# A normalise, shift and blur kernel whose second half takes its units in another order

## The chip, the cores and the metric

One core of one Trainium2 chip. The metric is the device time of one execution in microseconds (us), given as the median of several runs. Engines: TensorE (PE), VectorE (DVE), ScalarE (ACT), GpSimd (POOL), SyncE (SP).

## The reference

The input x is 32 images of 384 channels of 64 x 64 values in float32 (201 MB). It is normalised in groups of 12 channels, each channel group of 8 is moved by its own offset, blurred by a 3 x 3 kernel, and added to x:

```python
x = x + _L0_conv_ref(_gn(x), L0_conv_offset)
# _gn:   32 groups of 12 channels: (g - mean) / sqrt(var + 1e-5)
# _conv: off_round = round(offset); out = shift of each of 48 positions (8 channels) by off_round,
#        zeros where nothing comes in; then a depthwise 3x3 blur, its weights
#        exp(-(dx*dx + dy*dy) / 0.5), normalised, dx and dy from the offset's fraction
```

The 48 positions are a 7 x 7 grid of shifts, each 0, 16, 32 or 48 pixels up, down, left or right, without the centre. What remains of an image after a shift is a rectangle of (64 - |x|) x (64 - |y|) values, between 256 and 3072. Outside it (and its border) the output is x.

## The kernel before

**Tiles.** A tile is one position for 16 images: 128 partitions (16 images x 8 channels) of 4096 values, 2.10 MB. There are 48 positions and two halves of 16 images, so 96 tiles (`ALL`). SBUF holds 10 of them (`SLOTS`); tile n lies in slot n % 10, is loaded, updated in place and stored from there.

**Units.** The groups of 12 channels reach over the borders of positions; three neighbouring positions (24 channels) close two groups. So three tiles form a unit (`UNIT`), and a tile can't be normalised before all three tiles of its unit are loaded and summed. There are 16 units a half, 32 in all. A unit is named by its place in the program (units 16 to 31 are the second half).

**Order.** `positions_in_order` (L53) sorts the 16 units by the number of values that remain after the shift (`area`), takes the eight small and the eight large by turns, and swaps the last two. The list has 48 entries and both halves use it: places 0 to 47 and 48 to 95 (`ORDER[n % TILES]`). The sizes of its units, in order, each as the sizes of three tiles:

| place in the half | tiles | place | tiles |
|---|---|---|---|
| 0 | 256, 512, 768 | 8 | 1024, 768, 512 |
| 1 | 2304, 1536, 768 | 9 | 1024, 2048, 3072 |
| 2 | 768, 512, 256 | 10 | 1024, 512, 768 |
| 3 | 3072, 2304, 1536 | 11 | 1536, 2048, 1536 |
| 4 | 256, 512, 1024 | 12 | 768, 512, 1024 |
| 5 | 1536, 2304, 3072 | 13 | 1536, 2048, 1536 |
| 6 | 1024, 512, 256 | 14 | 768, 1536, 2304 |
| 7 | 3072, 2048, 1024 | 15 | 512, 768, 1024 |

**POOL** issues every load and store of x and out as an indirect DMA, with the rows from the table `row_of` (L182 to L202). It loads ten tiles, then for every n: wait until DVE has finished tile n, store it, wait until store n-1 has landed, load tile n+9 into that slot. All of these transfers go through one queue.

**ACT** (L226 on) makes two passes over each tile, the sum (L239) and the sum of squares about the mean (L243), except for tiles 0 and 2, which DVE sums; after the first tile of the next unit it takes the root for the unit before (L251), for which it waits for the matmuls of the variance.

**PE** adds the sums over the partitions of a group with a mask (L213): one set for the mean and one for the variance of each unit.

**DVE** does the rest of a tile, in `row_taps` (L380) and `column_tap` (L420): an edge to zero (L390), the normalised and shifted rectangle (L393), two row taps (L409, L414), and three column taps that add into the tile (L436, and L434 twice). Its time follows the size. In `run` (L439) the small steps of the next unit's statistics are placed among these:

```python
if j == UNIT - 2 and u < ALL_UNITS:
    spread_of_unit(u)
...
if j == UNIT - 1 and u < ALL_UNITS:
    scale_of_unit(u)
```

so in the second tile of a unit, after its first column tap, DVE waits for the next unit's means and makes the variance; and in the third tile, before its last tap, it waits for the root. A value read from memory sends the kernel down this branch when the offsets round to the planned grid, as they do here; the other branch (`displace`) serves other offsets.

Of the kernel before, what the change touches and what calls it, by code (L numbers as in the profile page):

```python
# [17 lines left out]
B, C, H, W = 32, 384, 64, 64  # L18
# [4 lines left out]
CH = C // POSITIONS  # L23
GROUP = C // 32
BT = 128 // CH
CHUNKS = B // BT
UNIT = 3
UNITS = POSITIONS // UNIT
TILES = UNITS * UNIT
# [6 lines left out]
SMALL = 7  # L36
MOVES = 1 + W + 2 + H
# [9 lines left out]
def planned_offsets():  # L47

    n = GRID // 2
    return [(ix * STRIDE, iy * STRIDE) for iy in range(-n, n + 1) for ix in range(-n, n + 1) if ix or iy]  # L50


def positions_in_order():  # L53

    def area(unit):
        return sum((W - abs(x)) * (H - abs(y)) for x, y in planned_offsets()[UNIT * unit:UNIT * (unit + 1)])

    units = sorted(range(UNITS), key=area)
    small, large = units[:UNITS // 2], units[UNITS // 2:]

    large = large[:1] + large[:1:-1] + large[1:2]
    order = [unit for pair in zip(small, large) for unit in pair]

    order[-2:] = order[:-3:-1]
    return [UNIT * unit + j for unit in order for j in range(UNIT)]


def span(shift, size):

    return max(0, shift), size + min(0, shift)  # L70
# [8 lines left out]
def norm_shift_blur(nc, x, offset, planned, steps, masks, rows, out):  # L79
    f32, i32, u32, u8 = mybir.dt.float32, mybir.dt.int32, mybir.dt.uint32, mybir.dt.uint8  # L80
    ALU = mybir.AluOpType
    ACT = mybir.ActivationFunctionType
    AX = mybir.AxisListType
    ORDER = positions_in_order()
    PLAN = planned_offsets()
    NP = POSITIONS
# [5 lines left out]
    with ctx:  # L92
# [169 lines left out]
        def _(dve):  # L262
# [77 lines left out]

            def scale_of_unit(u):

                par, base, p = u % 2, u * SMALL, ORDER[UNIT * u % TILES]

                dve.wait_ge(std_done, u + 1)
                nc.vector.reciprocal(rstd[:], std[:, par]).then_inc(small_done, 1)  # L346
                dve.wait_ge(small_done, base + 5)
                nc.vector.tensor_tensor(scale[:, par, :], rstd[:], middle[:, p:p + UNIT],  # L348
                                        ALU.mult).then_inc(small_done, 1)
                dve.wait_ge(small_done, base + 6)  # L350
                nc.vector.tensor_tensor(shift[:, par, :], scale[:, par, :], nmean[:],  # L351
                                        ALU.mult).then_inc(small_done, 1)

            def displace(n):

                g, t = normed, rowblur
                base, p = n * MOVES, ORDER[n % TILES]

                dve.wait_ge(col_taps, 1 + n * COL_TAPS)
                nc.vector.memset(t[:], 0.0).then_inc(moved, 1)  # L360
                with dve.Fori(0, W) as c:
                    to = dve.value_load(target[p:p + 1, 0, bass.ds(c, 1)], min_val=0, max_val=W + 1)

                    dve.wait_ge(moved, base + 1 + c)
                    nc.vector.tensor_scalar(t[:, :, bass.ds(to, 1)], g[:, 1:1 + H, bass.ds(c + 1, 1)], 1.0, None,
                                            ALU.mult).then_inc(moved, 1)

                dve.wait_ge(moved, base + 1 + W)
                nc.vector.memset(t[:, :, 0:W + 2:W + 1], 0.0).then_inc(moved, 1)
                nc.vector.memset(g[:], 0.0).then_inc(moved, 1)  # L370
                with dve.Fori(0, H) as r:
                    to = dve.value_load(target[p:p + 1, 1, bass.ds(r, 1)], min_val=0, max_val=H + 1)

                    dve.wait_ge(moved, base + 3 + W + r)
                    nc.vector.tensor_scalar(g[:, bass.ds(to, 1), :], t[:, bass.ds(r, 1), :], 1.0, None,
                                            ALU.mult).then_inc(moved, 1)

                dve.wait_ge(moved, base + MOVES)

            def row_taps(n, general):  # L380
                i, j = divmod(n, UNIT)
                p = ORDER[n % TILES]
                ox, oy = (0, 0) if general else PLAN[p]
                (xa, xb), (ya, yb) = span(ox, W), span(oy, H)
                image = tiles[:, n % SLOTS, :].rearrange("p (y x) -> p y x", x=W)

                dve.wait_ge(row_taps_done, 1 + n)
                if not general:
                    col = xa if xa > 0 else 1 + xb
                    nc.vector.memset(normed[:, 1 + ya:1 + yb, col:col + 1], 0.0).then_inc(edge_done, 1)  # L390

                dve.wait_ge(small_done, (i + 1) * SMALL)
                nc.vector.tensor_scalar(normed[:, 1 + ya:1 + yb, 1 + xa:1 + xb],  # L393
                                        image[:, ya - oy:yb - oy, xa - ox:xb - ox],
                                        scale[:, i % 2, j:j + 1], shift[:, i % 2, j:j + 1],
                                        ALU.mult, ALU.add).then_inc(normed_done, 1)
                dve.wait_ge(normed_done, n + 1)
                if general:
                    displace(n)
                else:  # L400
                    dve.wait_ge(edge_done, n + 1)
                g = normed[:, 1 + ya:1 + yb]
                t = rowblur[:, ya:yb]

                dve.wait_ge(col_taps, 1 + n * COL_TAPS)

                near = 1 if xb == W else -1
                ea, eb = max(0, xa - 1), min(W, xb + 1)
                nc.vector.scalar_tensor_tensor(t[:, :, 1 + ea:1 + eb], g[:, :, 1 + ea + near:1 + eb + near],  # L409
                                               ratio[:, (near + 1) // 2, p, 0:1], g[:, :, 1 + ea:1 + eb],  # L410
                                               ALU.mult, ALU.add).then_inc(first_row_tap, 1)
                fa, fb = max(0, xa + near), min(W, xb + near)
                dve.wait_ge(first_row_tap, n + 1)
                nc.vector.scalar_tensor_tensor(t[:, :, 1 + fa:1 + fb], g[:, :, 1 + fa - near:1 + fb - near],  # L414
                                               ratio[:, (1 - near) // 2, p, 0:1], t[:, :, 1 + fa:1 + fb],
                                               ALU.mult, ALU.add).then_inc(row_taps_done, 1)

                dve.wait_ge(row_taps_done, n + 2)

            def column_tap(n, general, nth):  # L420
                p = ORDER[n % TILES]
                ox, oy = (0, 0) if general else PLAN[p]
                (xa, xb), (ya, yb) = span(ox, W), span(oy, H)
                ea, eb = max(0, xa - 1), min(W, xb + 1)
                image = tiles[:, n % SLOTS, :].rearrange("p (y x) -> p y x", x=W)
                tap = (0, -1, 1)[nth]

                ra, rb = max(0, ya - tap), min(H, yb - tap)
                y = image[:, ra:rb, ea:eb]
                t = rowblur[:, ra + tap:rb + tap, 1 + ea:1 + eb]  # L430
                if nth:

                    dve.wait_ge(col_taps, 1 + n * COL_TAPS + nth)
                    ins = nc.vector.scalar_tensor_tensor(y, t, ratio[:, (tap + 1) // 2, p, 1:2], y, ALU.mult, ALU.add)  # L434
                else:
                    ins = nc.vector.tensor_tensor(y, t, y, ALU.add)  # L436
                ins.then_inc(col_taps, 1)

            def run(general):  # L439
                spread_of_unit(0)  # L440
                scale_of_unit(0)
                for n in range(ALL):
                    u, j = n // UNIT + 1, n % UNIT
                    row_taps(n, general)
                    column_tap(n, general, 0)
                    if j == UNIT - 2 and u < ALL_UNITS:
                        spread_of_unit(u)
                    column_tap(n, general, 1)
                    if j == UNIT - 1 and u < ALL_UNITS:
                        scale_of_unit(u)  # L450
                    column_tap(n, general, 2)
# [34 lines left out]
```

## Time and profile before

| | us |
|---|---|
| median of 3 runs | 989.47 |
| lowest, highest | 986.73, 991.32 |
| the profiled execution | 984.86 |
| its span | 983.1 |
| busy: DVE | 871.3 (89%) |
| busy: ACT | 714.3 (73%) |
| busy: POOL | 324.8 (33%) |
| busy: PE | 201.4 (20%) |
| read from and written to memory | 201.90 MB, 201.33 MB |
| mean rate over the span | 410 GB/s |

The span runs from the first to the last thing that the profiler records; times in the rows are from its start. An engine's busy time leaves out waits. POOL's busy time is the time in which it writes the descriptors of its DMAs; the transfer runs after that, and a row on a DMA issue doesn't show it. Transfers are seen in the DMA share and in GB/s.

### The profile page before, as it was taken

The page shows a single profiled execution, that of the slowest core. Times are in us where ns is not written, and L with a number is a line of the kernel's source. Part 1 is how long each engine was busy: PE and PEld are TensorE (multiplying, and loading weights), DVE is VectorE, ACT ScalarE, POOL GpSimd, SP SyncE. Part 2 cuts the span into 40 slices and gives each one's busy share as a digit, 9 for nine tenths or more (in the row PEclk, how much of TensorE's full clock was granted, in tenths as well). Part 3 has the DMA queues.
Part 4 walks back from the last instruction along what each step waited for, and adds up shares of the span by engine and source line. Part 5 has one row for each costly group of instructions (what it writes and reads, how often), then busy time and mean ns, then how long its engine had stood idle before and what let it go on. Part 6 is the DMA issues. An engine that isn't in the chain of part 4 may idle for free.

```text
span 983.1 us, 3636 instructions
## 1 busy us (share of the span) xinstructions
PE 201.4 (20%) x896; PEld 195.9 (20%) x896; DVE 871.3 (89%) x940; ACT 714.3 (73%) x412; POOL 324.8 (33%) x196
## 2 busy tenths in 40 slices
PE   0232222212122122122211221311212202222110
PEld 0221222212122122122211221311212202222110
DVE  4479899999999999999838949989999999979994
ACT  2998959777598777686777787686778777777800
POOL 3022342543323434223222317326141353223211
DMA  8999999999999999999999999999999999999966
GB/s 323 428 397 417 418 415 418 425 420 423 423 426 417 417 427 416 417 419 421 405 427 429 426 429 404 418 413 412 415 432 427 422 399 419 429 416 431 423 297 278
DMA packets 28233, 403.48 MB, mean 410 GB/s; under 512 B 3506, under 2 KB 3506, under 8 KB 3634
## 3 DMA queue, kind: packets, MB, share of 16 engines
q0 software_dynamic: 27648, 402.67, 98.2%
q1 hardware_dynamic: 562, 0.57, 0.2%
q8 instruction: 7, 0.11, 0.0%
q14 instruction: 16, 0.13, 0.0%
HBM read 201.90 MB, written 201.33 MB: 410 GB/s over the span
## 4 chain that ended last, share of the span: by engine, by line
DMA 54%; DVE 30%; issue 6%; POOL 5%; ACT 4%; PE 0%; POOLq 0%; ACTq 0%
DMA out<-tiles,row_of 48%; DVE tiles L434 10%; DMA tiles<-x,row_of 5%; DVE rowblur L409 5%; DVE tiles L436 5%; DVE rowblur L414 5%; POOL tiles L184 5%; ACT unread L239 3%; DVE normed L393 3%; ACT unread L243 1%; PE var_ps L213 0%; DMA row_of<-rows 0%; DVE scale L348 0%; DVE shift L351 0%; DVE apart L332 0%
## 5 line engine op out<-in xcount | busy, mean ns | idle before, releaser
L239 ACT ACTIVATE unread<-tiles 128x4096 uint8<-128x4096 f32 x94 | 339.9, 3616 | 165.2 <-DMA tiles<-x,row_of 164.7
L243 ACT ACTIVATE unread<-tiles,nmean_p 128x4096 uint8<-128x4096 f32 x94 | 348.7, 3709 | 3.0
L184 POOL DMA_INDIRECT tiles<-x,row_of x96 | 155.9, 1624 | 504.2 <-DMA out<-tiles,row_of 498.9
L434 DVE SCALAR_TENSOR_TENSOR tiles<-rowblur,ratio,tiles 128x272 f32<-128x272 f32 (+15 forms) x192 | 300.0, 1562 | 4.6
L213 PE MATMUL mean_ps<-nmean_p,mask 128*128 128x1 f32 x448 | 100.7, 353 | 567.3 <-ACT unread L239 537.2
L189 POOL DMA_INDIRECT out<-tiles,row_of x96 | 168.7, 1757 | 142.6 <-DVE tiles L434 119.7
L213 PEld LDWEIGHTS mean_ps<-nmean_p,mask 128*128 128x128 f32 x448 | 98.0, 330 | 570.0 <-ACT unread L239 539.8
L409 DVE SCALAR_TENSOR_TENSOR rowblur<-normed,ratio 128x272 f32<-128x272 f32 (+9 forms) x96 | 152.2, 1586 | 3.4
L436 DVE TENSOR_TENSOR tiles<-rowblur,tiles 128x272 f32<-128x272 f32 (+9 forms) x96 | 146.5, 1526 | 3.3
L414 DVE SCALAR_TENSOR_TENSOR rowblur<-normed,ratio,rowblur 128x240 f32<-128x240 f32 (+9 forms) x96 | 145.4, 1515 | 3.4
L213 PE MATMUL var_ps<-var_p,mask 128*128 128x1 f32 x448 | 100.7, 353 | 169.0 <-DVE var_p L338 169.0
L213 PEld LDWEIGHTS var_ps<-var_p,mask 128*128 128x128 f32 x448 | 98.0, 330 | 171.7 <-DVE var_p L338 171.7
L393 DVE TENSOR_SCALAR normed<-tiles,scale,shift 128x768 f32<-128x768 f32 (+6 forms) x96 | 87.3, 909 | 0.0
L251 ACT ACTIVATE std<-var_ps,eps 128x3 f32<-128x3 f32 x32 | 8.0, 252 | 50.8 <-PE var_ps L213 50.8
L329 DVE TENSOR_SCALAR nmean<-mean_ps 128x3 f32<-128x3 f32 x32 | 5.0, 155 | 37.2 <-PE mean_ps L213 37.2
L346 DVE RECIPROCAL rstd<-std 128x3 f32<-128x3 f32 x32 | 5.5, 171 | 27.1 <-ACT std L251 27.1
L312 DVE BATCH_NORM_STATS2 pieces<-tiles 128x6 f32<-128x512 f32 x16 | 9.7, 678 | 8.9 <-DMA tiles<-x,row_of 8.9
L239 ACT ACTIVATION_READ_ACCUMULATOR unread<-tiles 128x1 f32 x94 | 17.6, 187 | 0.0
L243 ACT ACTIVATION_READ_ACCUMULATOR unread<-tiles,nmean_p 128x1 f32 x94 | 17.5, 186 | 0.0
L390 DVE MEMSET normed<- 128x16 f32 (+3 forms) x96 | 8.5, 88 | 0.0
L338 DVE SCALAR_TENSOR_TENSOR var_p<-m_p,apart 128x3 f32<-128x3 f32 x32 | 5.2, 161 | 1.9 <-ACT unread L243 0.5
L351 DVE TENSOR_TENSOR shift<-scale,nmean 128x3 f32<-128x3 f32 x32 | 5.2, 164 | 1.1
(34 smaller groups left out, 25.9 us busy)
## 6 DMA issues: line engine op xcount, KB each, us to landing
tiles<-x,row_of POOLq DMA_INDIRECT x96, 14.9
out<-tiles,row_of POOLq DMA_INDIRECT x96, 17.6
mask<-masks SPq DMA_DIRECT2D x1, 448.0 KB, 3.2
row_of<-rows SPq DMA_DIRECT2D x1, 48.0 KB, 1.9
offs<-offset SPq DMA_DIRECT2D x1, 48.0 KB
plan_sb<-planned SPq DMA_DIRECT2D x1, 0.4 KB
offs_p<-offset SPq DMA_DIRECT2D x1, 0.4 KB
steps_sb<-steps SPq DMA_DIRECT2D x1, 12.0 KB
```

Source lines behind the costliest of these rows:

```text
L184: pool.indirect_dma_start(tiles[:, n % SLOTS, :], None, x_rows, bass.IndirectOffsetOnAxis(ap=row_of[:, n:n + 1], axis=0)).then_inc(loaded[ ...
L189: pool.indirect_dma_start(out_rows, bass.IndirectOffsetOnAxis(ap=row_of[:, n:n + 1], axis=0), tiles[:, n % SLOTS, :], None).then_inc(store ...
L213: last = nc.tensor.matmul(ps[:, k:k + 1], mask[:, PAIRS.index((j, k)), :], src[:, j:j + 1], start=(j == from_[0]), stop=(j == from_[-1]))
L239: nc.scalar.activation(unread[:], tiles[:, n % SLOTS, :], ACT.Identity, scale=-1.0 / HW, accum_out=nmean_p[:, i % 2, j:j + 1]).then_inc(nm ...
L243: nc.scalar.activation(unread[:], tiles[:, n % SLOTS, :], ACT.Square, bias=nmean_p[:, i % 2, j:j + 1], accum_out=m2_p[:, i % 2, j:j + 1]). ...
L312: nc.vector.bn_stats(pieces[:, e, :], tile[:, e, :]).then_inc(pieces_done, 1)
L390: nc.vector.memset(normed[:, 1 + ya:1 + yb, col:col + 1], 0.0).then_inc(edge_done, 1)
L393: nc.vector.tensor_scalar(normed[:, 1 + ya:1 + yb, 1 + xa:1 + xb], image[:, ya - oy:yb - oy, xa - ox:xb - ox], scale[:, i % 2, j:j + 1], s ...
L409: nc.vector.scalar_tensor_tensor(t[:, :, 1 + ea:1 + eb], g[:, :, 1 + ea + near:1 + eb + near], ratio[:, (near + 1) // 2, p, 0:1], g[:, :, ...
L414: nc.vector.scalar_tensor_tensor(t[:, :, 1 + fa:1 + fb], g[:, :, 1 + fa - near:1 + fb - near], ratio[:, (1 - near) // 2, p, 0:1], t[:, :, ...
L434: ins = nc.vector.scalar_tensor_tensor(y, t, ratio[:, (tap + 1) // 2, p, 1:2], y, ALU.mult, ALU.add)
L436: ins = nc.vector.tensor_tensor(y, t, y, ALU.add)
```

## The change

The second half gets a list of its own. The large units come in falling order of size, each followed by a small one, also falling; the last two large ones (4608 values each) come one after the other, and the two smallest (1536 each) are last. In the order of places 16 to 31 the tiles are: 1536, 2304, 3072; 512, 768, 1024; 3072, 2304, 1536; 768, 512, 1024; 1024, 2048, 3072; 1024, 512, 768; 3072, 2048, 1024; 1024, 768, 512; 1536, 2048, 1536; 1024, 512, 256; 1536, 2048, 1536; 256, 512, 1024; 768, 1536, 2304; 2304, 1536, 768; 768, 512, 256; 256, 512, 768. The list returned has 96 entries, so the modulo goes, and the table of rows is made from the same list. The first half is as before. The added lines shift the line numbers below them by 3.

```diff
@@ -62,6 +62,9 @@
     order = [unit for pair in zip(small, large) for unit in pair]
 
     order[-2:] = order[:-3:-1]
+
+    small, large = small[::-1], sorted(large, key=area)[::-1]
+    order += [unit for pair in zip(large[:-2], small[:-2]) for unit in pair] + large[-2:] + small[-2:]
     return [UNIT * unit + j for unit in order for j in range(UNIT)]
...
-                par, base, p = u % 2, u * SMALL, ORDER[UNIT * u % TILES]
+                par, base, p = u % 2, u * SMALL, ORDER[UNIT * u]
...
             def row_taps(n, general):
                 i, j = divmod(n, UNIT)
-                p = ORDER[n % TILES]
+                p = ORDER[n]
...
             def column_tap(n, general, nth):
-                p = ORDER[n % TILES]
+                p = ORDER[n]
...
-        "rows": np.stack([(chunk * BT + batch) * C + CH * p + ch for chunk in range(CHUNKS)
-                          for p in positions_in_order()], axis=1).astype(np.uint32),
+        "rows": np.stack([(n // TILES * BT + batch) * C + CH * p + ch
+                          for n, p in enumerate(positions_in_order())], axis=1).astype(np.uint32),
```

(`displace` is changed like `row_taps`.)

What moves on DVE, at the two places of which the prediction speaks. First the start of the second half, tile 48 and the start of tile 49, before and then after the change (the last number is the shape: partitions x rows x columns):

```order
L390 MEMSET normed 128x16
L393 TENSOR_SCALAR normed<-tiles,scale,shift 128x16x16
L409 SCALAR_TENSOR_TENSOR rowblur<-normed,ratio 128x16x17
L414 SCALAR_TENSOR_TENSOR rowblur<-normed,ratio,rowblur 128x16x15
L436 TENSOR_TENSOR tiles<-rowblur,tiles 128x16x17
L434 SCALAR_TENSOR_TENSOR tiles<-rowblur,ratio,tiles 128x16x17
L434 SCALAR_TENSOR_TENSOR tiles<-rowblur,ratio,tiles 128x15x17
```

```order
L393 MEMSET normed 128x48
L396 TENSOR_SCALAR normed<-tiles,scale,shift 128x48x32
L412 SCALAR_TENSOR_TENSOR rowblur<-normed,ratio 128x48x33
L417 SCALAR_TENSOR_TENSOR rowblur<-normed,ratio,rowblur 128x48x31
L439 TENSOR_TENSOR tiles<-rowblur,tiles 128x48x33
L437 SCALAR_TENSOR_TENSOR tiles<-rowblur,ratio,tiles 128x48x33
L437 SCALAR_TENSOR_TENSOR tiles<-rowblur,ratio,tiles 128x47x33
```

The same six steps and the memset stand there; a tile of 256 values a partition has given its place to one of 1536, and 2304 and 3072 follow where 512 and 768 did. Second the end of DVE's list, from the last tap of tile 92 into tile 93, before and after:

```order
L348 TENSOR_TENSOR scale<-rstd,middle 128x3
L351 TENSOR_TENSOR shift<-scale,nmean 128x3
L434 SCALAR_TENSOR_TENSOR tiles<-rowblur,ratio,tiles 128x48x49
L390 MEMSET normed 128x16
L393 TENSOR_SCALAR normed<-tiles,scale,shift 128x16x32
L409 SCALAR_TENSOR_TENSOR rowblur<-normed,ratio 128x16x33
```

```order
L351 TENSOR_TENSOR scale<-rstd,middle 128x3
L354 TENSOR_TENSOR shift<-scale,nmean 128x3
L437 SCALAR_TENSOR_TENSOR tiles<-rowblur,ratio,tiles 128x16x17
L393 MEMSET normed 128x16
L396 TENSOR_SCALAR normed<-tiles,scale,shift 128x16x16
L412 SCALAR_TENSOR_TENSOR rowblur<-normed,ratio 128x16x17
```

Tile 92 was one of 2304 (48 x 48) and is one of 256 (16 x 16); tile 93 was one of 512 and is one of 256. The small steps of the last unit's statistics stand before the last tap of tile 92 as they did. ACT, PE and POOL have the same instructions in the same order; only the rows in the table that POOL's transfers use are others.

## Rows read from the trace of the kernel before

**Rows 1.** The page: busy time by engine, GB/s in 40 slices, the POOL-issued queue

```profile
PE 201.4 (20%) x896; PEld 195.9 (20%) x896; DVE 871.3 (89%) x940; ACT 714.3 (73%) x412; POOL 324.8 (33%) x196
...
GB/s 323 428 397 417 418 415 418 425 420 423 423 426 417 417 427 416 417 419 421 405 427 429 426 429 404 418 413 412 415 432 427 422 399 419 429 416 431 423 297 278
...
q0 software_dynamic: 27648, 402.67, 98.2%
```

**Rows 2.** Waits: who waited for whom, in total, times, longest, POOL on the queue

```profile
POOL tiles L184 <- DMA out<-tiles,row_of: 498.9, 86, 9.4
```

**Rows 3.** Windows of the tail: stretch, busy by engine, clock, DMA share, GB/s

```profile
930.00:945.00 15.00, 6.29 (x28) 6.12 (x28) 14.69 (x14) 4.05 (x3) 1.95 (x1) 1.00 1.02 435
947.00:955.00 8.00, 0.00 (x0) 0.00 (x0) 7.83 (x10) 0.00 (x0) 1.01 (x1) 1.00 0.08 33
955.00:970.00 15.00, 0.00 (x0) 0.00 (x0) 14.54 (x18) 0.00 (x0) 2.43 (x2) 1.00 0.99 419
970.00:977.00 7.00, 0.00 (x0) 0.00 (x0) 0.57 (x1) 0.00 (x0) 0.95 (x1) 1.00 0.71 300
```

**Rows 4.** Timeline of POOL's last stores: start, duration, what, idle before and releaser

```profile
953.48 1.01 POOL L189 DMA_INDIRECT out<-tiles,row_of  x1 [13.12 <-DVE tiles L434]
...
970.85 0.95 POOL L189 DMA_INDIRECT out<-tiles,row_of  x1 [5.91 <-DVE tiles L434]
```

**Rows 5.** Timeline of DVE, the step that opens a tile (L393), second half

```profile
496.16 0.39 DVE L393 TENSOR_SCALAR normed<-tiles,scale,shift 128x256 f32<-128x256 f32 x1
...
583.81 1.83 DVE L393 TENSOR_SCALAR normed<-tiles,scale,shift 128x3072 f32<-128x3072 f32 x1
...
617.95 1.03 DVE L393 TENSOR_SCALAR normed<-tiles,scale,shift 128x1536 f32<-128x1536 f32 x1
...
628.60 0.40 DVE L393 TENSOR_SCALAR normed<-tiles,scale,shift 128x256 f32<-128x256 f32 x1
...
707.44 1.81 DVE L393 TENSOR_SCALAR normed<-tiles,scale,shift 128x3072 f32<-128x3072 f32 x1
...
748.11 0.80 DVE L393 TENSOR_SCALAR normed<-tiles,scale,shift 128x1024 f32<-128x1024 f32 x1
...
766.43 0.74 DVE L393 TENSOR_SCALAR normed<-tiles,scale,shift 128x1024 f32<-128x1024 f32 x1
```

**Rows 6.** Timeline of POOL's stores: third tile of units 16, 18, 22

```profile
542.82 1.58 POOL L189 DMA_INDIRECT out<-tiles,row_of  x1 [0.30 <-issue]
...
604.55 3.11 POOL L189 DMA_INDIRECT out<-tiles,row_of  x1 [0.30 <-issue]
...
724.24 3.71 POOL L189 DMA_INDIRECT out<-tiles,row_of  x1 [0.30 <-issue]
```

**Rows 7.** Timeline of POOL: a store that waited for DVE in the first half

```profile
266.05 1.28 POOL L189 DMA_INDIRECT out<-tiles,row_of  x1 [4.30 <-DVE tiles L434]
```

**Rows 8.** Timeline of DVE and ACT: statistics of units 29 and 31

```profile
874.09 0.16 DVE L329 TENSOR_SCALAR nmean<-mean_ps 128x3 f32<-128x3 f32 x1 [3.86 <-PE mean_ps L213]
...
933.75 0.15 DVE L329 TENSOR_SCALAR nmean<-mean_ps 128x3 f32<-128x3 f32 x1
...
937.78 0.26 ACT L251 ACTIVATE std<-var_ps,eps 128x3 f32<-128x3 f32 x1 [4.00 <-PE var_ps L213]
```

**Rows 9.** Timeline of DVE, the step that opens a tile, tail

```profile
938.11 1.43 DVE L393 TENSOR_SCALAR normed<-tiles,scale,shift 128x2304 f32<-128x2304 f32 x1
...
953.14 0.53 DVE L393 TENSOR_SCALAR normed<-tiles,scale,shift 128x512 f32<-128x512 f32 x1
...
957.50 0.66 DVE L393 TENSOR_SCALAR normed<-tiles,scale,shift 128x768 f32<-128x768 f32 x1
...
963.32 0.80 DVE L393 TENSOR_SCALAR normed<-tiles,scale,shift 128x1024 f32<-128x1024 f32 x1
```

**Rows 10.** Timeline of POOL's loads: the slowest stretch of the second half, first and last

```profile
589.88 3.46 POOL L184 DMA_INDIRECT tiles<-x,row_of  x1 [7.48 <-DMA out<-tiles,row_of]
...
642.60 0.97 POOL L184 DMA_INDIRECT tiles<-x,row_of  x1 [9.44 <-DMA out<-tiles,row_of]
```

More of the change, by code:

```diff
@@ L356, in displace @@
                 g, t = normed, rowblur
-                base, p = n * MOVES, ORDER[n % TILES]
+                base, p = n * MOVES, ORDER[n]
                 dve.wait_ge(col_taps, 1 + n * COL_TAPS)
```

## The prediction

> 0.5% of the time, about 5 us, is what a measurement of this kernel can tell from no change: the three runs of before spread from 986.73 to 991.32 us.
>
> **What bounds the kernel now.** I read the page first. VectorE (DVE) is busy 871.3 us (89%), yet the queue that GpSimd (POOL) fills moves 402.67 MB and its packets take 98.2% of the 16 DMA engines' span, and the rate holds between 397 and 432 GB/s from the second slice on until it falls to 297 and 278 in the last two [rows 1]. So the reader should see two things: the transfers set the pace, and only the end leaves them idle. The waits agree: POOL spends 498.9 us, in 86 pieces, waiting for stores to land before it may reload their slot [rows 2]. POOL's last load falls within this pace, and from 930 us the queue holds stores alone. Cut finely, the tail reads: 435 GB/s until 945, 33 GB/s from 947 to 955 while DVE is busy 7.83 of 8 us, 419 from 955 to 970, 300 from 970 to 977 [rows 3]. The hole is one large tile: POOL stood 13.12 us before it could issue the store at 953.48, because DVE was on a tile of 2304 elements a partition from 938.11 to 953.14 [rows 4, 9]. The last store, at 970.85, again waited 5.91 us for DVE [rows 4]. At the end, therefore, DVE is the bound; before it, the queue.
>
> **The change, part by part.**
>
> *Work added or removed: none.* Each half holds the same 48 tiles; each load and each store is 2.10 MB whatever the position; DVE's durations depend on the tile alone. The indices ORDER[n] are folded into the code when it is built. The statistics, the matmuls and POOL's list read the same, so everything rests on when DVE finishes a tile against when the queue wants it.
>
> *The tail.* What the queue still has to carry at 947 is four stores and the end of a fifth: 8.0 x 33 + 15.0 x 419 + 7.0 x 300 = 8.65 MB [rows 3]. At 435 GB/s that takes 19.9 us and ends at 966.9; at 419 it takes 20.6 and ends at 967.6. Now it ends at 977, so a queue without gaps ends 9.4 to 10.1 us earlier. The 6 us between the last byte and the end of the span stay. I take 10.0, since the nearest row with several stores queued at once is the one at 435.
>
> Is the data there in time? DVE's sums for unit 29 come out at 874.09 in the second tile of unit 28, paced by loads that don't move [rows 8]. DVE waits there before and after (the ledger below lets it arrive sooner). From there: 0.8 of small steps and two column taps. A tile of 1536 takes 10.65 (617.95 to 628.60) of which 1.03 is the first step, so five equal taps are 1.92 each [rows 5]: 874.1 + 0.8 + 3.8 = 878.7. Then, in the new order, with 15.0 for 2304, 10.65 for 1536, 5.8 for 768, 4.4 for 512 and at most as much for 256 [rows 5, 9], and 0.7 for each set of small steps: unit 28's 2304 ends at 893.7; unit 29 (2304, 1536, 768) at 908.7, 920.1, 926.6; unit 30 (768, 512, 256) at 932.4, 937.5, 942.6; unit 31 (256, 512, 768) at 947.0, 951.4, 957.2. The last unit's statistics don't hold this up: its mean is there at 933.75, and the root was ready at 937.78, 4 us later [rows 8]; here the variance step falls near 936, the root near 940, before the last tap of tile 92 needs it. Store by store, with 1.3 for POOL's wake and issue, the data is ready at 943.9, 948.3, 952.7 and 958.5. Backwards from 966.9 in steps of 4.8 (2.10 MB at 435) the queue wants tiles 92 to 95 at 947.5, 952.4, 957.2 and 962.0. The least margin is 3.5 us, so the tail fills.
>
> *The middle.* The second half now begins with a unit of 6912 elements a partition (1536, 2304, 3072), and has the heavier part of its work early. I keep a ledger. DVE starts on tile 48 at 496.16. A unit of 6912 takes 44.8 us (583.81 to 628.60), one of 6144 takes 40.7 (707.44 to 748.11), a small one of 2304 takes 18.3 (748.11 to 766.43) [rows 5]; unit 15 before them costs nothing new. That gives, for the end of the large units: 541.0, then 541.0 + 18.3 + 44.8 = 604.1, then + 18.3 + 40.7 = 663.1, then + 59.0 = 722.1. POOL's stores of the same tiles were issued, at the queue's pace, at 542.82, 604.55 and 724.24 (first, second and fourth) [rows 6]. The ledger is ahead by 1.8, 0.4 and 2.1 us. Units 23 to 27 hold 2304 + 5120 + 1792 + 5120 + 1792 = 16128 elements, at 6.85 ns (63.1 us for 9216) 110.4 us, against 15 pairs of transfers, 144 us or more: the lead grows again, and DVE would be in the second tile of unit 28 from some 845 on, well before the sums at 874.09.
>
> What if the ledger is late? POOL issues store n, waits for store n-1 to land, loads n+9. Stores land one pair of transfers apart, 9.6 us at 435 GB/s. A store up to that late delays no load, and the queue still holds a load and a store. The first half shows it: POOL waited 4.30 us for DVE before the store at 266.05 [rows 7] in slices of 423 and 426 GB/s [rows 1]. So I cost the middle at nothing; the cover is 9.6 us over the ledger, and each us beyond it would be a us lost. Where DVE idles now between 490 and 585, waiting for sums of small units, it will not; none of that was on the path, since the queue ran on.
>
> *POOL's issues.* DVE now has large tiles from 496 on. A load issue took 0.97 us at 642.60 and 3.46 at 589.88 [rows 10], beside DVE's large unit. The count of such tiles is unchanged, and POOL waited 7.48 and 9.44 us before those two [rows 10], which absorbs it, so I cost it at nothing. The Trainium skill (SBUF — State Buffer, SBUF: two separate sides) says that a DVE instruction that holds the port pair shared with GpSimd keeps it from writing descriptors, so that the DMA engines sit idle. The trace agrees with the longer issues and not, in the steady part, with idle engines (98.2% busy). By the rows the term is 0; by that rule alone each issue beside a large tile would leave the engines idle for the 2.5 us more that it takes, 40 us for 16 of them, and the change would lose; rival D is its mechanism.
>
> **Sum.** The profiled execution took 984.86 us, span 983.1: 984.86 - 10.0 = 974.9. It lies 4.6 below the median of the three runs, 989.47, against which I predict: 979.5 us.
>
> **The rivals.**
>
> *A, the forecast:* tail filled, middle unharmed. For it: the margins above. 979.5, and 975 to 984.5 with 4 us of the queue's own unevenness either way. Chance 0.64.
>
> *B, the middle runs dry a little.* A wait for statistics comes in at units 17 to 22 that the ledger, at 0.4 us, has no room for. ACT and DVE depend on each other there: ACT waits for the matmuls of the variance before it goes on to the next sums. The wait at 874.09 was 3.86 us [rows 8]; if one four times as long, 15 us, falls at tile 56, it is 5 us beyond the cover, and the gain shrinks to 5 or less: 984.5 to 989. Against it: that wait was for loads, which DVE had outrun, and here it lags. Chance 0.18.
>
> *C, more than the sum.* The 18 slices from 492 to 934 average 421 GB/s [rows 1], 10.0 us a pair of transfers where 435 makes 9.6; over 45 pairs that is some 15 us. If the queue is fed more evenly because DVE no longer sprints and stalls, half of it could come back: 972. Nothing in the rows shows such a link. Chance 0.10.
>
> *D, slower: POOL is kept from writing descriptors.* From the load at 589.88 to that at 642.60 there are 5 pairs in 52.7 us, 10.5 each, during DVE's unit of 6912 [rows 10]. If that is the price of a large unit that follows another closely, 0.9 us a pair over 9.6, and all of tiles 48 to 72 (24 pairs) pay it where before about a third did, it is 16 x 0.9 = 14 us; with twice that price, 28. So 989.5 - 10 + 14 = 993.5, up to 1007.5. It takes the whole gain from 10 us on, 0.6 us a pair over those 16, and is slower by over 0.5% from 15 on. Against it: the slice from 713 to 737, beside another large unit, shows 432 GB/s [rows 1], and POOL's long store at 724.24 (3.71) [rows 6] cost no rate. The mechanism is the one of the rule named above. Chance 0.06.
>
> *E, the change does not do what it says.* The list has 96 entries, the row table uses the same list, and the instruction order on DVE changes at tile 48 as told; only if the check of the offsets sent the kernel down its general branch would it not matter, and the trace shows it does not. Chance 0.02, at 989.5.
>
> **Numbers.** The likeliest gives 979.5. Faster by over 0.5% (below 984.5): A, C and a little of B, 0.76. Within 0.5%: most of B, E: 0.17. Slower: D and a tail of E, 0.07. The range takes A and half of C below and B above: 973 to 989.
>
> **What would show it.** Right: DMA share near 1.00 up to about 967 with no window under 400 GB/s after 930; POOL's last stores waiting for DVE no more than some 5 us each, and issued well ahead of the queue; the large tile's 13.12 us wait gone; DVE without idle time between 496 and 745; the span near 973. The ledger is right if POOL's stores of units 16, 18 and 22 wait for DVE 0 to 5 us. Wrong: windows below 400 GB/s between 540 and 740 with POOL waiting over 10 us for DVE (B), the same with POOL's issues long and DVE done (D), or a gap in the last 40 us, which would put the fault in the tail's list of tiles.

## The result and the profile after

The changed kernel takes 978.82 us (median of 13 runs, 976.50 to 984.16); the kernel before takes 986.71 us in 13 runs beside them (980.60 to 991.32). The ratio on record is 0.9934, with a 95% interval from 0.9915 to 0.9953: faster by 0.7%, 6.5 us. (It is not the quotient of the medians, which lie 7.9 us apart; here and below the two differ by up to some 0.001.) The forecast of 979.5 us is met, but partly by luck: it was 10 us under a median of 989.47, which three runs on the high side had given. As a ratio it was 0.990, just outside the interval.

The page of the changed kernel, in the lines that answer to [rows 1]:

```profile
PE 201.4 (21%) x896; PEld 195.9 (20%) x896; DVE 871.0 (89%) x940; ACT 714.3 (73%) x412; POOL 326.6 (33%) x196
...
GB/s 358 428 368 421 420 422 414 424 404 395 415 426 411 405 423 412 424 421 429 429 424 419 417 415 416 421 407 429 418 419 419 417 428 427 422 431 406 428 429 280
...
q0 software_dynamic: 27648, 402.67, 99.0%
```

DVE's work is the same (871.0 us). The rate no longer drops in the last slice but one (429 instead of 297 GB/s) and the queue's share went from 98.2 to 99.0%. The waits (engine line waited for: us in total, times, longest), to [rows 2]:

```profile
POOL tiles L187 <- DMA out<-tiles,row_of: 512.6, 85, 8.9
...
POOL out L192 <- DVE tiles L437: 85.3, 16, 24.6
```

The second line read like this before:

```profile
POOL out L189 <- DVE tiles L434: 119.7, 21, 27.2
```

POOL waits less for DVE than before, 85.3 us instead of 119.7, and a little longer for the queue (512.6 against 498.9). The tail in windows (stretch, busy time of PE, PEld, DVE, ACT, POOL, granted clock, DMA share, GB/s), to [rows 3]:

```profile
930.00:945.00 15.00, 6.29 (x28) 6.12 (x28) 14.26 (x34) 5.08 (x5) 3.92 (x4) 1.00 1.01 430
945.00:955.00 10.00, 0.00 (x0) 0.00 (x0) 8.03 (x11) 0.00 (x0) 2.10 (x2) 1.00 1.01 433
955.00:965.00 10.00, 0.00 (x0) 0.00 (x0) 0.00 (x0) 0.00 (x0) 0.00 (x0) 1.00 1.01 431
965.00:970.00 5.00, 0.00 (x0) 0.00 (x0) 0.00 (x0) 0.00 (x0) 0.00 (x0) 1.00 0.61 262
970.00:977.00 7.00, 0.00 (x0) 0.00 (x0) 0.00 (x0) 0.00 (x0) 0.00 (x0) 1.00 0.02 7
```

The hole is gone. What the forecast did not have is in the last two rows: the queue does not stop at a stroke near 967, it thins out until 972. Last, POOL's last load and two of its last stores in the timeline (start, duration, what, idle before and releaser), to [rows 4]:

```profile
912.80 1.82 POOL L187 DMA_INDIRECT tiles<-x,row_of  x1 [5.56 <-DMA out<-tiles,row_of]
...
940.49 0.95 POOL L192 DMA_INDIRECT out<-tiles,row_of  x1 [2.32 <-DVE tiles L437]
...
953.59 0.95 POOL L192 DMA_INDIRECT out<-tiles,row_of  x1 [4.67 <-DVE tiles L437]
```

The store of tile 92, which stood 13.12 us before, waited 2.32. The start of the last load is a good mark, because what remains to be moved from there on is the same in every order: this load, what was already queued, and the stores behind it. Before the change it was issued here:

```profile
911.58 0.97 POOL L184 DMA_INDIRECT tiles<-x,row_of  x1 [5.29 <-DMA out<-tiles,row_of]
```

From this mark to the end of the span the kernel before takes 983.1 - 911.6 = 71.5 us, the changed one 976.7 - 912.8 = 63.9: **the tail is 7.6 us shorter**. The two profiled executions differ by 6.4 us in all, because the changed one reached the mark 1.2 us later.

The ledger of the middle can be read from DVE's opening steps, to [rows 5]: the start of the half, then the tile behind each of the four large units,

```profile
497.29 1.03 DVE L396 TENSOR_SCALAR normed<-tiles,scale,shift 128x1536 f32<-128x1536 f32 x1
...
542.09 0.53 DVE L396 TENSOR_SCALAR normed<-tiles,scale,shift 128x512 f32<-128x512 f32 x1
...
605.22 0.63 DVE L396 TENSOR_SCALAR normed<-tiles,scale,shift 128x768 f32<-128x768 f32 x1
...
664.57 0.78 DVE L396 TENSOR_SCALAR normed<-tiles,scale,shift 128x1024 f32<-128x1024 f32 x1
...
723.88 0.80 DVE L396 TENSOR_SCALAR normed<-tiles,scale,shift 128x1024 f32<-128x1024 f32 x1
```

and from POOL's stores, to [rows 6]: those of the third tiles of units 16, 18 and 20, tile 67, and the third of unit 22:

```profile
544.64 1.12 POOL L192 DMA_INDIRECT out<-tiles,row_of  x1 [0.30 <-issue]
...
606.40 1.39 POOL L192 DMA_INDIRECT out<-tiles,row_of  x1 [0.30 <-issue]
...
665.77 1.76 POOL L192 DMA_INDIRECT out<-tiles,row_of  x1 [0.30 <-issue]
...
716.42 1.28 POOL L192 DMA_INDIRECT out<-tiles,row_of  x1 [1.85 <-DVE tiles L437]
...
725.83 1.00 POOL L192 DMA_INDIRECT out<-tiles,row_of  x1 [0.30 <-issue]
```

From the start at 497.29 the large units end 44.8, 107.9, 167.3 and 226.6 us later; the ledger had 44.8, 107.9, 166.9 and 225.9. POOL's stores of these tiles were issued 1.2 to 2.6 us after DVE had ended them, so DVE stayed ahead; one other store, at 716.42, waited 1.85 us for DVE. DVE itself waited for nothing between 496 and 745 us.

### The profile page after: what moved, and what is told of

Same layout as the page of the kernel before. It is cut to its first block, busy times and chain, and to the rows that moved or that the text cites. A ratio compares the mean times of both kernels' runs of the same rounds, so it can differ in the third digit from the quotient of the medians.

```text
span 976.7 us, 3636 instructions
## 1 busy us (share of the span) xinstructions
PE 201.4 (21%) x896; PEld 195.9 (20%) x896; DVE 871.0 (89%) x940; ACT 714.3 (73%) x412; POOL 326.6 (33%) x196
## 4 chain that ended last, share of the span: by engine, by line
DVE 48%; DMA 39%; issue 5%; ACT 4%; POOL 3%; POOLq 0%; ACTq 0%; DVEq 0%
DMA out<-tiles,row_of 30%; DVE tiles L437 17%; DVE rowblur L412 8%; DMA tiles<-x,row_of 8%; DVE tiles L439 8%; DVE rowblur L417 8%; DVE normed L396 5%; POOL tiles L187 3%; ACT unread L242 3%; ACT unread L246 1%; DVE scale L351 0%; DVE shift L354 0%; DVE var_p L341 0%; DVE apart L335 0%; DVE apart L337 0%
## 5 line engine op out<-in xcount | busy, mean ns | idle before, releaser
L187 POOL DMA_INDIRECT tiles<-x,row_of x96 | 156.8, 1633 | 518.0 <-DMA out<-tiles,row_of 512.6
L437 DVE SCALAR_TENSOR_TENSOR tiles<-rowblur,ratio,tiles 128x735 f32<-128x735 f32 (+24 forms) x192 | 300.0, 1562 | 4.6
L192 POOL DMA_INDIRECT out<-tiles,row_of x96 | 169.7, 1768 | 109.6 <-DVE tiles L437 85.3
L412 DVE SCALAR_TENSOR_TENSOR rowblur<-normed,ratio 128x784 f32<-128x784 f32 (+14 forms) x96 | 152.2, 1586 | 3.4
L439 DVE TENSOR_TENSOR tiles<-rowblur,tiles 128x784 f32<-128x784 f32 (+14 forms) x96 | 146.5, 1526 | 3.3
L417 DVE SCALAR_TENSOR_TENSOR rowblur<-normed,ratio,rowblur 128x752 f32<-128x752 f32 (+14 forms) x96 | 145.5, 1515 | 3.4
L396 DVE TENSOR_SCALAR normed<-tiles,scale,shift 128x768 f32<-128x768 f32 (+7 forms) x96 | 87.4, 910 | 0.0
L393 DVE MEMSET normed<- 128x16 f32 (+3 forms) x96 | 8.5, 88 | 0.0
```

Source lines behind the costliest of these rows:

```text
L187: pool.indirect_dma_start(tiles[:, n % SLOTS, :], None, x_rows, bass.IndirectOffsetOnAxis(ap=row_of[:, n:n + 1], axis=0)).then_inc(loaded[ ...
L192: pool.indirect_dma_start(out_rows, bass.IndirectOffsetOnAxis(ap=row_of[:, n:n + 1], axis=0), tiles[:, n % SLOTS, :], None).then_inc(store ...
```

## The experiments

The experiments test theory T: the gain is the closed hole in the tail, it is limited by the queue, and the middle does nothing. Against it stood rival M (the middle brings part), L (large units early cost something), and S (the tail has the full 10 us and the change doesn't reach them). Times are medians. Each ratio is to runs of the kernel before that stood beside the experiment, with its 95% interval.

**Only the tail (e1, e6).** The list that the change appends, replaced:

```diff
-    order += [unit for pair in zip(large[:-2], small[:-2]) for unit in pair] + large[-2:] + small[-2:]
+    order += [14, 6, 11, 10, 2, 5, 13, 8, 1, 7, 4, 12, 3, 9, 15, 0]
```

> The second half keeps small units first, and only its end is the new one (units of 5120, 4608, then 1536 and 1536). Theory T, the whole gain is the closed hole in the tail and the middle is neutral: ratio to the kernel before 0.993, the same as the change, 6 to 7 us less. Rival M, the large units early bring part of the gain: ratio 0.996 to 1.000. Rival L, the large units early cost something that hides part of the tail's 10 us: ratio 0.990, about 3 us better than the change. In the profile all of them expect the rate to hold at 420 GB/s or more from 930 to 965.

Measured 972.4 us against 982.25: 0.9912 (0.9885 to 0.9938). The tail alone brings the whole gain, so rival M (0.996 to 1.000) falls. The interval holds T's 0.993 and L's 0.990 alike. (e6 is the same kernel again, below.)

**Only the front (e2).** The same line replaced by another list, with the old units at its end:

```diff
+    order += [5, 4, 10, 1, 7, 13, 8, 2, 12, 15, 6, 0, 11, 3, 9, 14]
```

> The second half begins with large units by turns as in the change, but ends with the old units (5120, 4608, 2304). Theory T: ratio 1.000, a hole of some 8 us before the store of the 2304-element tile comes back. Rival M: ratio 0.993 to 0.997. Rival L: ratio 1.003 or more, with the lead of DVE over POOL's stores used up near tiles 55 to 68.

Measured 979.23 us against 982.25: 0.9978 (0.9957 to 0.9999). T's 1.000 lies just outside the interval, L's 1.003 well outside. POOL's last load and the store of tile 92 in its timeline:

```profile
907.48 2.10 POOL L186 DMA_INDIRECT tiles<-x,row_of  x1 [6.06 <-DMA out<-tiles,row_of]
...
948.70 1.01 POOL L191 DMA_INDIRECT out<-tiles,row_of  x1 [13.12 <-DVE tiles L436]
```

The hole is back: a wait of 13.12 us again, and from the last load to the end of the span (978.3) 70.8 us. So most of the gain is gone without the new tail.

**DVE's work in the tail left out (e3 from the kernel before, e4 from the changed one).** In `row_taps` and `column_tap`:

```diff
                 (xa, xb), (ya, yb) = span(ox, W), span(oy, H)
+                if n >= 88 and not general:
+                    yb = ya + 2
```

> The kernel before, but on tiles 88 to 95 DVE works on 2 rows of each rectangle only, so it leaves out nearly all of the work there and no store of the tail waits for it. This is the floor that the queue sets for the old order. Theory T: ratio 0.993, as the change, because the 10 us of my sum can't be had: each of the 16 DMA engines carries an equal share and one that is some 5 us behind ends the span. Rival S, the sum's 10 us were there and the change only leaves 3 of them: ratio 0.990 or less.

> The changed kernel with the same work left out (tiles 88 to 95, 2 rows each). Theory T: ratio 0.993 as the change, since its tail is already at the queue's floor; the profile's last landings are spread over some 5 us. Rival S: ratio 0.990, 3 us better than the change, since DVE would still be holding stores back.

Measured 975.25 us, 0.9937 (0.9911 to 0.9962), for e3 and 974.7 us, 0.9928 (0.9896 to 0.9960), for e4. With hardly any work for DVE in the tail, the old order is as fast as the change (0.9934) and the change gets nothing more; S had expected 0.990 or less. The stretch from the last load to the end says it without much of the scatter of whole runs. The last column is how far apart the 16 DMA engines reported their parts of the very last store, of which more below. All thirteen profiled executions are here (e5 and e11 are the changed kernel again; e7 to e10 come below):

| kernel | last load at | span | from there to the end | last store, first to last report |
|---|---|---|---|---|
| before | 911.6 | 983.1 | 71.5 | 1.1 |
| e2, only the front | 907.5 | 978.3 | 70.8 | 1.1 |
| changed | 912.8 | 976.7 | 63.9 | 5.6 |
| changed, again (e5) | 906.0 | 969.9 | 63.9 | 6.3 |
| changed, again (e11) | 906.2 | 970.1 | 63.9 | 5.8 |
| e1, only the tail | 903.8 | 967.7 | 63.9 | 4.2 |
| e6, only the tail, again | 905.8 | 970.0 | 64.2 | 5.8 |
| e3, before, work left out | 916.2 | 980.1 | 63.9 | 6.0 |
| e4, changed, work left out | 909.7 | 973.5 | 63.9 | 6.9 |
| e9, changed, work left out from tile 12 | 894.7 | 958.5 | 63.8 | 6.2 |
| e10, changed, pause in the middle | 916.6 | 979.7 | 63.1 | 5.3 |
| e8, changed, earlier first store | 910.1 | 972.4 | 62.3 | 4.2 |
| e7, changed, pause near the end | 911.2 | 977.7 | 66.5 | 1.1 |

With the queue full to the end the tail takes 62.3 to 64.2 us, in most executions 63.9, whether DVE has work there or not. This is what the queue sets, and it is not quite one number. Rival S falls: leaving out DVE's work gains nothing over the change. The tail is worth 7.6 us (6.9 from e2; 9.2 against the shortest one), not 10.

**A pause in the queue near the end (e7), and in the middle (e10).** The forecast's tail would have taken 71.5 - 10.0 = 61.5 us. Why does it take 63.9? Here are single microseconds of the changed kernel's end, then of the kernel before's:

```profile
965.00:966.00 1.00, 0.00 (x0) 0.00 (x0) 0.00 (x0) 0.00 (x0) 0.00 (x0) 1.00 0.96 410
...
967.00:968.00 1.00, 0.00 (x0) 0.00 (x0) 0.00 (x0) 0.00 (x0) 0.00 (x0) 1.00 0.65 279
...
969.00:970.00 1.00, 0.00 (x0) 0.00 (x0) 0.00 (x0) 0.00 (x0) 0.00 (x0) 1.00 0.23 98
...
971.00:972.00 1.00, 0.00 (x0) 0.00 (x0) 0.00 (x0) 0.00 (x0) 0.00 (x0) 1.00 0.04 16
```

```profile
975.00:976.00 1.00, 0.00 (x0) 0.00 (x0) 0.00 (x0) 0.00 (x0) 0.00 (x0) 1.00 0.65 279
976.00:977.00 1.00, 0.00 (x0) 0.00 (x0) 0.00 (x0) 0.00 (x0) 0.00 (x0) 1.00 1.23 516
977.00:978.00 1.00, 0.00 (x0) 0.00 (x0) 0.00 (x0) 0.00 (x0) 0.00 (x0) 1.00 0.05 16
```

The end of the kernel before is sharp, 516 GB/s and then 16; the changed one's takes 5 us to fade. The trace also has the moment when each of the 16 DMA engines reports its part of a transfer. In these two executions 4 to 5.5 us lie between the first and the last of them while the queue is full, and 5.6 for the changed kernel's last store; for the last store before the change, which came after the hole, it is 1.1. So each engine has a part of every transfer, they are apart while the queue is full, and the latest one ends the span, which closes 4.3 us after its report in both. Near the end the last engine's reports come some 4.85 us apart, one store after the other. The changed kernel has two steps of 5.65 among them, to its reports at 961.96 and 967.60; e10 has one and e8 none, and their tails are 63.9, 63.1 and 62.3 us. So these steps account for what lies between the three; why an engine falls back there is open. The width alone does not set the tail either: e1's last reports were 4.2 us apart like e8's, and its tail is 63.9.

If the late engines use a hole to catch up, a hole is partly paid for. To test this, a pause was added to the changed kernel, at the store of tile 92:

```diff
                 pool.wait_ge(col_taps, 1 + (n + 1) * COL_TAPS)
+                if n == 92:
+                    pool.wait_ge(stored[(n - 1) % SLOTS], landed(n - 1))
```

> The changed kernel, and POOL waits before the store of tile 92 until the store of tile 91 has landed, so the queue runs dry once, near 950 us, some 5 us long. Theory T (16 engines that drift apart by 4 to 6 us while the queue is full; a pause lets the late ones catch up): the last bytes end within about 1 us of each other instead of thinning out over 5, and the pause costs 0 to 3 us: ratio 0.993 to 0.996. Rival S (a pause is lost in full): ratio 0.998 to 1.000, 5 to 7 us more than the change.

> The changed kernel once more, beside the next three on one chip. Theory T: ratio to the kernel before 0.993 (0.991 to 0.996). It is the yardstick for the others.

Measured 976.83 us (0.9953, 0.9926 to 0.9981) with the pause and 976.77 us (0.9946, 0.9915 to 0.9977) for the changed kernel beside it. Windows of e7:

```profile
946.00:949.00 3.00, 0.00 (x0) 0.00 (x0) 2.90 (x5) 0.00 (x0) 0.00 (x0) 1.00 0.37 158
949.00:952.00 3.00, 0.00 (x0) 0.00 (x0) 2.74 (x3) 0.00 (x0) 1.05 (x2) 1.00 0.01 3
952.00:971.00 19.00, 0.00 (x0) 0.00 (x0) 0.00 (x0) 0.00 (x0) 2.77 (x3) 1.00 1.01 426
971.00:972.00 1.00, 0.00 (x0) 0.00 (x0) 0.00 (x0) 0.00 (x0) 0.00 (x0) 1.00 0.65 279
972.00:973.00 1.00, 0.00 (x0) 0.00 (x0) 0.00 (x0) 0.00 (x0) 0.00 (x0) 1.00 0.04 16
```

The queue runs down from 946 and is empty from 949 to 952, the rate is above 400 GB/s behind that, and the end is sharp. From 942 to 962 us the queue moved 6.3 MB; in the changed kernel, at 430 GB/s, the same 20 us moved 8.6, so the pause left out about 5 us of transfer. From the last load to the end it takes 66.5 us, 2.6 more than the changed kernel (4.2 more than e8). Over whole runs the pause can't be told from none, as theory T said, though the intervals would hide some 3 to 4 us; S's 0.998 lies at the edge of the interval. The same at tile 60, where POOL also waits for the load in flight:

```diff
+                if n == 60:
+                    pool.wait_ge(stored[(n - 1) % SLOTS], landed(n - 1))
+                    pool.wait_ge(loaded[(n + 8) % SLOTS], landed(n + 8))
```

> The changed kernel, and POOL waits once, at tile 60, until all transfers in flight have landed, before it goes on. The same kind of pause as the one near 950 us, but in the middle. If late DMA engines catch up in a pause and only the end of the span shows how late they are, this one is lost as they drift apart again: 3 to 6 us more than the change, ratio 0.997 to 1.000. If a pause costs nothing wherever it is (the queue makes it good later): ratio 0.994 as the change.

> The changed kernel as the yardstick on this chip: ratio 0.993 to 0.995.

Measured 980.97 us, 0.9997 (0.9971 to 1.0023), against 973.69 us, 0.9931 (0.9901 to 0.9961), for the changed kernel: 7 us lost, against a forecast of 3 to 6. This pause was the bigger one. In POOL's timeline of e10 the store at 653.15 waited 14.46 us, and the load at 675.63 waits again:

```profile
653.15 3.47 POOL L192 DMA_INDIRECT out<-tiles,row_of  x1 [14.46 <-DMA tiles<-x,row_of]
...
675.63 0.98 POOL L187 DMA_INDIRECT tiles<-x,row_of  x1 [10.45 <-DMA out<-tiles,row_of]
```

Between 648 and 672 us the queue moved 6.0 MB, where 419 GB/s make 10.1: about 10 us of transfer were left out. From the load of tile 53 to that of tile 95 the execution took 428.0 us; the five executions of this order that leave nothing out and have no pause there took 416.9 to 421.7. So the pause in the middle cost 6 to 11 us of some 10, the one near the end 2.6 (or 4.2) of some 5. The two are not of one size, and one execution stands for each, so this is support and no proof. What the trace does show is the engines drifting apart anew: the reports of one transfer lie 4.1 us apart before the pause of e10, 0.2 right after it, about 1 until 695 us, 3.1 at 712 and 4.0 at 742. At the start of the changed kernel it is the same: 1.2 us apart until 51 us, 4.5 at 136.

**Do large units early cost something?** e6 repeats e1 beside e5.

> The order with only the tail changed, once more. Theory T (only the tail counts): the same as the changed kernel, ratio 0.993, and the 0.991 seen before was scatter. Rival L (large units early cost 2 us): ratio 0.991 again, and 0.002 under the changed kernel on the same chip.

Measured 971.82 us, 0.9912 (0.9879 to 0.9946): the same as e1, and 5 us under the changed kernel on the same chip (976.77). Windows of the first third of the half, for before, changed, and e6:

```profile
490.00:645.00 155.00, 31.48 (x140) 30.62 (x140) 119.67 (x142) 117.58 (x70) 53.39 (x32) 1.00 1.01 422
```

```profile
490.00:645.00 155.00, 31.48 (x140) 30.62 (x140) 150.03 (x137) 117.25 (x68) 57.10 (x31) 1.00 1.01 418
```

```profile
490.00:645.00 155.00, 31.45 (x140) 30.60 (x140) 131.89 (x148) 117.93 (x68) 45.65 (x31) 1.00 1.01 427
```

With large units early the rate is 418 GB/s, with e6's order, small ones first, 427: over 155 us that is 3 us. But the rest gives part of it back. From the load of tile 53 to that of tile 95 the order of e1 and e6 took 416.5 and 417.7 us, the changed kernel 418.6, 419.3 and 418.1, and e2 418.2: some 1 to 2 us apart, where e7 and e8, with the changed kernel's order, took 421.7 and 416.9. And e2, with large units early and the old tail, should then be slower than before, and was 0.2% faster. So rival L is neither shown nor excluded: the order of e1 had the lower ratio both times, but the intervals overlap, and the traces give it 1 to 2 of the 5 us.

**DVE's work left out from tile 12 on (e9).** The edit of e4 with `n >= 12`.

> The changed kernel, but from tile 12 on DVE works on 2 rows of each rectangle only; it leaves out most of its work, all transfers and sums stay. It asks whether a busy DVE lowers the rate of the queue (POOL's issues wait while DVE's large instructions run). Theory P, it does: POOL's issues take 1.0 us instead of 1.6 and 1.8 on average, the rate between 120 and 930 us rises from 420 to 426 GB/s or more, and the time falls by 12 us or more against the change: ratio 0.982 or less. Rival N, the rate's 2 to 3% under its best are the transfers' own: the rate stays at 418 to 422, ratio 0.990 to 0.994.

Measured 959.69 us, 0.9766 (0.9737 to 0.9796). From 120 to 930 us, e9 and then the changed kernel:

```profile
120.00:930.00 810.00, 176.24 (x784) 171.43 (x784) 197.92 (x801) 616.75 (x356) 172.45 (x168) 1.00 1.01 429
```

```profile
120.00:930.00 810.00, 169.66 (x756) 165.03 (x755) 762.68 (x758) 611.46 (x350) 288.35 (x162) 1.00 1.01 419
```

and POOL's loads in the page, e9 and then the changed kernel (busy us, mean ns of one | idle before):

```profile
L187 POOL DMA_INDIRECT tiles<-x,row_of x96 | 105.9, 1103 | 618.4 <-DMA out<-tiles,row_of 612.9
```

```profile
L187 POOL DMA_INDIRECT tiles<-x,row_of x96 | 156.8, 1633 | 518.0 <-DMA out<-tiles,row_of 512.6
```

Theory P's forecasts are met: the queue runs at 429 GB/s beside a mostly idle DVE (24% busy) and at 419 beside a busy one, some 19 us in 810, and POOL's load issues fall from 1633 to 1103 ns. What links the two is not separated: DVE's accesses and POOL's longer issues went away together. The Trainium skill (SBUF — State Buffer, Who interferes with whom) says that DMA never contends with a compute engine, and that one which seems stalled by VectorE is a GpSimd-issued one, short of descriptors. The issue times agree with that. But the DMA share is 1.01 in both rows, so the engines do not look starved; what changed is the single packet. In the same 810 us a packet of 16 KB took 614 ns on the mean in e9 and 628 in the changed kernel, 2.3% more, and that is about the whole difference of the rates. A hint that it is not DVE's busy time alone stands in the windows above: before the change DVE was less busy than in e6 (119.67 against 131.89 us), and yet the rate was lower (422 against 427), with POOL busier (53.39 against 45.65).

**An earlier first store (e8).** In `run`:

```diff
-                    if j == UNIT - 2 and u < ALL_UNITS:
+                    if j == (UNIT - 1 if u == 1 else UNIT - 2) and u < ALL_UNITS:
```

> The changed kernel, and at the very start the variance of unit 1 is made in tile 2 instead of tile 1, so that DVE doesn't hold tile 1 until 55 us. The second store can then go at some 45 us and the first reload at 59 instead of 64, and the dip of the rate to 350-375 GB/s between 60 and 75 us is filled. If the queue is the bound all through: 3 us less than the change, ratio 0.990. If the start is bound elsewhere (DVE then stands in tile 2 for as long): no difference, 0.993.

Measured 975.37 us, 0.9944 (0.9917 to 0.9970): no difference from the changed kernel beside it (e5, 0.9946), as the second of the two forecasts had it. The second store went at 44.26 instead of 52.79 us, but the first reload was issued at 62.94 (62.30 in the changed kernel), since it waits for the first store to land behind ten loads. The start is bound by that.

## Why the prediction was right, and where it was off

- **What bounds the kernel:** right. The queue sets the pace, and in the second half only the tail had DVE holding it up.
- **The data is there in time:** right, with room to spare. The last tile was done at 953.3 (forecast 957.2; a tile of 256 took 2.9 us, where the sum had put the 4.4 of a tile of 512). e4 shows that nothing is left to gain from DVE there.
- **The tail, 10.0 us:** this is the term that was mis-sized. It measured 7.6. "At 435 GB/s that takes 19.9 us and ends at 966.9" took 16 engines for one. The rate did hold to 965, but then faded, because the engines were up to 5.6 us apart, while the old tail, after its hole, ended with all of them together. The last packet ended at 972.0, and 1.2 us of that are the later mark: 970.8 on the clock of the kernel before, 3.9 us after the 966.9 of the sum. The other way, "Now it ends at 977" was 1.3 us early, as the kernel before has packets until 978.3. 10.1 - 3.9 + 1.3 = 7.5.
- **"The 6 us between the last byte and the end of the span stay":** they do stay, but they are 4.7 to 4.8 (978.3 to 983.1 before, 972.0 to 976.7 after). The 6 came from the same early 977.
- **The middle at nothing:** right. The ledger was within 0.7 us at its four marks, and the one wait of 1.85 us lay inside the cover. B and D's loss did not happen. From the load of tile 53 to that of tile 95 the two profiled executions took 419.8 and 418.6 us.
- **POOL's issues at nothing:** right for this change, since the whole run holds the same work. The reason given, that POOL's waiting absorbs longer issues, is not tested by it. e9 shows 2% of the rate lost beside a busy DVE, spread over the whole run before and after. If that goes through POOL's issues, the reason was wrong; it may not, and the DMA engines were as busy in both, so it is not the idle engines of rival D.
- **C, a gain in the middle:** not seen in the change. The traces of e1 and e6 hint at 1 or 2 us of it for another order.

Of the kernels that leave nothing out, e1 (and e6) has the lowest ratio, 0.9912 of the kernel before; its interval overlaps that of the changed kernel.

## What to carry to other kernels

Where transfers bound a kernel and compute only has to keep up, look at what compute holds back behind the last load, and put the smallest pieces of work there. Don't price the tail as bytes over rate: measure from the last load to the end, and find what the queue allows by leaving out the compute, in more than one profiled execution, as it differed by up to 2 us here. A hole shortly before the end cost less than its length here (7.6 us for some 10 of transfer left out before the change, 2.6 for some 5 in e7).

## What had not been expected of the hardware

- The 16 DMA engines report their parts of one transfer 4 to 5.5 us apart when the queue is full (before and changed; in other executions 3 to 6, and up to 6.9 at the end of e4), and 0.2 to 1.2 us apart after a pause. After the pause of e10 it took some 80 us until they were 4 us apart again.
- A queue whose DMA share stays at 1.01 carries 429 GB/s beside a VectorE that is busy 24% of the time and 419 to 420 beside one that is busy 92 to 94% of the time, and the mean 16 KB packet takes 614 and 628 ns.
- The part of the program up to tile 47 is the same in all these kernels but e8 and e9, yet the load of tile 53, which follows from it, was issued between 486.7 and 494.7 us in the 11 profiled executions. That scatter is larger than that of the tail and makes much of the difference between whole runs.
